# First graph convolution: own-row bias folded into the weights, and another order of work on TensorE, ScalarE and VectorE

## The reference

```python
x = _layernorm(x + _L0_gnn_ref(x, edge_weight, src, dst, ...))
x = _layernorm(x + _L1_gnn_ref(x, edge_index, edge_weight1, ...))   # two transformer convolutions
x = _layernorm(x + _L2_gnn_ref(...))
x = _layernorm(x + _L3_gnn_ref(...))
```

```python
q = (x @ qw + qb).reshape(N, HEADS, CH)          # 8 heads of 16
k = (x @ kw + kb).reshape(N, HEADS, CH)
v = (x @ vw + vb).reshape(N, HEADS, CH)
alpha = jnp.sum(q[dst] * k[src], axis=-1) * SCALE
m = jax.ops.segment_max(alpha, dst, num_segments=N)
a = jnp.exp(alpha - m[dst])
denom = jax.ops.segment_sum(a, dst, num_segments=N)
a = a / denom[dst]
msg = v[src] * a[:, :, None]
out = jax.ops.segment_sum(msg, dst, num_segments=N).reshape(N, HEADS * CH)
return out + x @ sw + sb                          # followed by relu
```

## Time and profile before

| | |
|---|---|
| median of 3 runs (lowest to highest) | 3210.21 us (3208.09 to 3211.15) |
| the profiled execution: own time, span | 3208.55 us, 3206.6 us |
| granted TensorE clock, mean over the span | 0.903 |
| first convolution, 720 to 1190 us: VectorE busy | 454.83 of 470 us |
| the same: TensorE, ScalarE, GpSimd busy | 431.81, 285.16, 166.08 us |
| the same: granted clock, DMA share, GB/s | 1.00, 0.65, 196 |

### The profile page before, as it was taken

One profiled execution on the slowest core, in us unless ns is written; L12 is line 12 of the kernel. 1 busy time (PEld: TensorE's weight loads), 2 busy tenths in 40 slices (PEclk: granted clock), 3 DMA queues, 4 the chain that ended last, 5 costly groups with the idle time before them and its releaser, 6 DMA issues. The chain is left out here.

```text
span 3206.6 us, 46374 instructions
## 1 busy us (share of the span) xinstructions
PE 2528.0 (79%) x14129; PEld 1744.9 (54%) x14129; DVE 2643.1 (82%) x3326; ACT 2089.0 (65%) x3677; POOL 1868.2 (58%) x1771
## 2 busy tenths in 40 slices
PE   7899999959999987888888699999999752445500
PEld 3466666636666654666666466776777541224400
DVE  6599999969999996999999557988888756999910
ACT  0167677636665656999999589999999753555500
POOL 4477777623333326777776466555555007777776
PEclk9999999979999998999999899999999855667855
DMA  7356676656666656777777347889888548885211
GB/s 212 110 187 218 216 228 219 210 166 201 197 200 196 200 169 187 235 232 234 233 230 227 112 144 196 216 208 224 216 220 205 152 113 258 277 276 146 84 40 39
DMA packets 495087, 611.79 MB, mean 191 GB/s; under 512 B 66865, under 2 KB 284651, under 8 KB 494716
## 3 DMA queue, kind: packets, MB, share of 16 engines
q1 hardware_dynamic: 433030, 495.63, 51.3%
q0 software_dynamic: 56480, 111.88, 13.1%
q10 hardware_dynamic: 5334, 1.32, 0.2%
HBM read 391.94 MB, written 220.55 MB: 191 GB/s over the span
## 5 line engine op out<-in xcount | busy, mean ns | idle before, releaser
L775 POOL DMA_INDIRECT c_xs<-table_x,src_row x196 | 185.0, 944 | 302.6 <-PE c_psT L916 249.4
L1815 POOL DMA_INDIRECT f_rows<-table_x,src_row x196 | 227.8, 1162 | 227.8 <-POOLq L1216 168.4
L1295 POOL DMA_INDIRECT g_xd_xs<-table_x,dst_row x196 | 200.0, 1021 | 260.9 <-PE g_psT L1363 167.5
L765 POOL DMA_INDIRECT c_xs<-table_h,src_row x196 | 221.3, 1129 | 121.2 <-issue 78.9
L497 POOL DMA_INDIRECT xs<-in_x,src_i x196 | 227.1, 1159 | 86.6 <-issue 55.5
L482 POOL DMA_INDIRECT xd<-in_x,dst_i x196 | 216.5, 1104 | 94.0 <-issue 47.9
L1295 POOL DMA_INDIRECT g_xd_xs<-table_x,src_row x196 | 206.5, 1053 | 59.7 <-issue 59.7
L1822 POOL DMA_INDIRECT out<-f_rows,end_i x196 | 197.4, 1007 | 62.4 <-issue 62.4
L1867 PE MATMUL f_psT<-w_ident,f_rows 128*128 128x128 f32 x196 | 48.9, 397 | 219.9 <-DVE f_rows L1960 219.9
L765 POOL DMA_INDIRECT c_xd<-table_h,dst_row x196 | 185.0, 944 | 59.7 <-issue 59.7
L1368 PEld LDWEIGHTS g_psP<-w_center,g_turns 128*128 128x128 f32 x1568 | 185.2, 193 | 49.8 <-ACT g_turns L1504 28.5
(11 more groups left out here) (330 smaller groups left out, 8588.6 us busy)
## 6 DMA issues: line engine op xcount, KB each, us to landing
g_share<-shares SPq DMA_DIRECT2D x196, 192.0 KB
xn<-in_x SPq DMA_DIRECT2D x49, 512.0 KB
table_x<-xo SPq DMA_DIRECT2D x49, 512.0 KB, 2.9
table_x1b<-xb SPq DMA_DIRECT2D x49, 512.0 KB, 4.9
c_xn<-table_x SPq DMA_DIRECT2D x49, 512.0 KB
table_h<-c_xo SPq DMA_DIRECT2D x49, 512.0 KB
c_xn<-table_h SPq DMA_DIRECT2D x49, 512.0 KB
c_x1r<-table_x1b SPq DMA_DIRECT2D x49, 512.0 KB
```

Source lines behind the costliest of these rows:

```text
L765: pool.indirect_dma_start(out=quarters(rows[:, s, :])[j], out_offset=None, in_=table, in_offset=edge_index(columns, now.n, j)).then_inc(la ...
L775: pool.indirect_dma_start(out=quarters(xs[:, s, :])[j], out_offset=None, in_=table, in_offset=edge_index(h.src_row, now.n, j)).then_inc(sr ...
L1295: pool.indirect_dma_start(out=quarters(xd_xs[:, s, k, :])[j], out_offset=None, in_=table, in_offset=edge_index(columns, now.n, j)).then_in ...
L1815: pool.indirect_dma_start(out=quarters(rows[:, n, :])[j], out_offset=None, in_=table, in_offset=edge_index(h.src_row, n, j)).then_inc(src_ ...
```

## The change

Own-row bias. A constant 1.0 is added to every value of the turned node rows (`bias=1.0` in the copy out of PSUM), and the own-row weight becomes `s0_lifted` = `s0` + (`s_b0` - column sums of `s0`) / 128. Since every row that the convolution reads has mean zero, (x + 1) @ `s0_lifted` is x @ `s0` + `s_b0`. VectorE's two additions and the array `pre` go; ScalarE takes the relu straight out of PSUM, one half at a time (`store_nodes`), half 0 in the tile's own step and half 1 in the next. The set-up gets one matmul (column sums) and two small VectorE operations for the new weight.

Order. On TensorE q comes right behind the first turn, the edge rows of tile n - 2 move behind k, the own rows of half 0 ahead of the turn of half 1, the scores ahead of the values, and the own rows of half 1 to the end. On VectorE `kq` moves ahead of `pv`, `den` and `num`. ScalarE's step becomes a function of its own. SyncE and GpSimd keep their order; SyncE's store now waits for both halves. In `layer2` the first of two adjacent matmuls now counts as well, and the two waits on it count double.

```diff
@@ setup, VectorE and TensorE
+            dve.wait_ge(columns_summed, 1)
+            link(nc.vector.tensor_tensor(h.s_b0[:, :], h.s_b0[:, :], psm[:, P:2 * P], ALU.subtract))
+            link(nc.vector.scalar_tensor_tensor(out=h.s0_lifted[:, :], in0=h.s_b0[:, :], scalar=1.0 / P,
+                                                in1=h.w["s0"][:, :], op0=ALU.mult, op1=ALU.add))
...
+            pe.wait_ge(loaded, n_loads[0])
+            nc.tensor.matmul(psm[:, P:2 * P], ones[:, :], h.w["s0"][:, :], start=True, stop=True).then_inc(columns_summed, 1)
@@ conv, SyncE
-                    sp.wait_ge(out_ready, last.n + 1)
+                    sp.wait_ge(out_ready, 2 * last.n + 2)
@@ conv, TensorE
-                wait(pe, pren_ready, 2 * now.n - 1 + k)
+                wait(pe, pren_ready if layer else out_ready, 2 * now.n - 1 + k)
...
-                    if soon:
-                        turn_dst(soon)
-                if old:
-                    edge_products(old)
                 if now:
                     pe.wait_ge(d_filled, now.n + 1)
                     wait(pe, kq_ready, now.n)
                     nc.tensor.matmul(psQ[:, :], w_q[:, :], xdT[:, now.at(t_slots), :],
                                      start=True, stop=True).then_inc(q_ready, 1)
+                if soon and now:
+                    turn_dst(soon)
+                if now:
                     turn_spread(1, now, xn[:, s, 0, :], node_landed[s], 16 * (now.half + 1))
                     pe.wait_ge(q_sb, now.n + 1)
                     nc.tensor.matmul(psQ[:, :], w_k[:, :], xsT[:, s, :], start=True, stop=True).then_inc(k_ready, 1)
+                if old:
+                    edge_products(old)
+                if now:
+                    own_rows(now, 0)
                     turn_spread(2, now, xn[:, s, 1, :], node_landed[s], 16 * (now.half + 1))
-                    own_rows(now, 0)
+                    alike(now)
                     values(now)
                     own_rows(now, 1)
-                    alike(now)
@@ conv, ScalarE
+            def keep_nodes(now, k):
+                act.wait_ge(turned, 3 * now.n + 2 + k)
+                wait(act, en_ready, 2 * now.n - 3 + k)
+                nc.scalar.activation(xnT[:, now.slot, k, :], psT[0][:, :], ACT.Copy, bias=1.0).then_inc(turned_sb, 1)
+
+            def store_nodes(tile, k):
+                act.wait_ge(en_ready, 2 * tile.n + 1 + k)
+                wait(act, node_stored[tile.slot], 16 * tile.half)
+                nc.scalar.activation(xo[:, tile.slot, k, :], psE[k][:, :], ACT.Relu).then_inc(out_ready, 1)
...
-                    act.wait_ge(pren_ready, 2 * now.n + 2)
-                    wait(act, node_stored[s], 16 * now.half)
-                    nc.scalar.activation(xo[:, s, 0:2, :], pre[:, s, 0:2, :], ACT.Relu).then_inc(out_ready, 1)
@@ conv, VectorE (times_q holds the old code of kq; for layer 1 it stays where it was)
+                if spread and now:
+                    times_q(now)
...
-                    for k in range(2):
-                        dve.wait_ge(en_ready, 2 * now.n + 1 + k)
-                        nc.vector.tensor_tensor(by_row(pre[:, now.slot, k, :]), by_row(psE[k][:, :]),
-                                                s_bias[:, :].rearrange("p (o f) -> p o f", o=1).to_broadcast([P, 4, P]),
-                                                ALU.add).then_inc(pren_ready, 1)
```

More of the change, by code:

```diff
@@ L792, in conv @@
         to_rows = h.w["ident"] if layer == 0 else h.w["center"]
-        s_bias = h.s_b0 if layer == 0 else h.s_b1c
+        w_own = h.s0_lifted if layer == 0 else h.s1c
         b_q, b_k, b_v = h.col(f"q_b{layer}"), h.col(f"k_b{layer}"), h.b_vs[:, layer:layer + 1]
@@ L930, in own_rows @@
                 pe.wait_ge(turned_sb, per_tile * (now.n + 1) - 1 + k)
-                wait(pe, pren_ready, 2 * now.n - 1 + k)
+                wait(pe, pren_ready if layer else out_ready, 2 * now.n - 1 + k)
                 for o, x in zip(quarters(psE[k]), quarters(xnT[:, now.slot, k, :])):
-                    ins = nc.tensor.matmul(o, x, w_s[:, :], start=True, stop=True)
+                    ins = nc.tensor.matmul(o, x, w_own[:, :], start=True, stop=True)
                 ins.then_inc(en_ready, 1)
@@ L1032, in step, with step_spread @@
+            def step_spread(t):
+                now, last, old = t.tile(0), t.tile(1), t.tile(2)
+                if now:
                     act.wait_ge(turned, 3 * now.n + 1)
                     wait(act, v_ready, now.n - 1)
-                    nc.scalar.activation(xsT[:, s, :], psT[0][:, :], ACT.Copy).then_inc(turned_sb, 1)
-                elif now:
+                    nc.scalar.activation(xsT[:, now.slot, :], psT[0][:, :], ACT.Copy).then_inc(turned_sb, 1)
+                    keep_q(now)
+                if last:
+                    store_nodes(last, 1)
+                if now:
+                    keep_nodes(now, 0)
+                if last:
+                    act.wait_ge(u_ready, last.n + 1)
+                    wait(act, pv_ready, last.n)
+                    wait(act, den_ready, last.n)
+                    nc.scalar.activation(p[:, :], u[:, :], ACT.Exp).then_inc(p_ready, 1)
+                    act.wait_ge(dropm_ready, last.n + 1)
+                    wait(act, num_ready, last.n)
+                    nc.scalar.activation(c[:, :], dropm[:, :], ACT.Exp).then_inc(c_ready, 1)
+                if old:
+                    keep_edges(old)
+                if now:
+                    store_nodes(now, 0)
+                    keep_nodes(now, 1)
+                if last:
+                    act.wait_ge(den_ready, last.n + 1)
+                    wait(act, rden_ready, last.n)
+                    nc.scalar.activation(lnd[:, :], den[:, last.slot, :], ACT.Ln).then_inc(lnd_ready, 1)
+                    act.wait_ge(lnd_ready, last.n + 1)
+                    wait(act, agg_ready, last.n)
+                    nc.scalar.activation(rden[:, :], lnd[:, :], ACT.Exp, scale=-1.0).then_inc(rden_ready, 1)
@@ L1036, in step @@
+            def step(t):
+                now, last, (g, a, b) = t.tile(0), t.tile(1), t.group(1)
+                if now:
                     s = now.slot
@@ L1043, in step @@
                         nc.scalar.activation(dst, psT[k][:, :], ACT.Copy).then_inc(turned_sb, 1)
-                if layer and g:
+                if g:
                     if a == 0:
@@ L1063, in step @@
                     nc.scalar.activation(p[:, :], u[:, :], ACT.Exp).then_inc(p_ready, 1)
-                if spread and old and not now:
-                    keep_edges(old)
                 if now:
                     for k in range(2):
-                        act.wait_ge(turned, per_tile * (now.n + 1) - 1 + k)
+                        act.wait_ge(turned, 4 * now.n + 3 + k)
                         wait(act, en_ready, 2 * now.n - 3 + k)
-                        nc.scalar.activation(xnT[:, s, k, :], psT[0 if spread else k][:, :],
-                                             ACT.Copy).then_inc(turned_sb, 1)
-                if layer and g:
+                        nc.scalar.activation(xnT[:, s, k, :], psT[k][:, :], ACT.Copy).then_inc(turned_sb, 1)
+                if g:
                     norm_scale(nc, act, h, g, a, b, var, lnv, rstd, var_ready, lnv_ready, rstd_ready, out_ready)
@@ L1083, in step @@
                     nc.scalar.activation(rden[:, :], lnd[:, :], ACT.Exp, scale=-1.0).then_inc(rden_ready, 1)
-                if layer and g:
+                if g:
                     scale_rows(t, g, a, b, 3, 12).then_inc(out_ready, 1)
-                if now and not layer:
-                    act.wait_ge(pren_ready, 2 * now.n + 2)
-                    wait(act, node_stored[s], 16 * now.half)
-                    nc.scalar.activation(xo[:, s, 0:2, :], pre[:, s, 0:2, :], ACT.Relu).then_inc(out_ready, 1)
-            run_steps(2, step)
+            run_steps(2, step_spread if spread else step)
         @block.vector
@@ L1112, in _, with times_q @@
                 fill_dst(Tile(0, 0))
+            def times_q(now):
+                dve.wait_ge(k_ready, now.n + 1)
+                dve.wait_ge(q_sb, now.n + 1)
+                wait(dve, a_ready, now.n)
+                nc.vector.scalar_tensor_tensor(out=kq[:, :], in0=psQ[:, :], scalar=b_k, in1=q[:, :],
+                                               op0=ALU.add, op1=ALU.mult).then_inc(kq_ready, 1)
             def add_x1(t, g, k):
@@ L1176, in step @@
                                                  ALU.mult, ALU.add).then_inc(num_ready, 1)
[L1177 to L1182, removed]
+                if now and not spread:
+                    times_q(now)
                 if last:
@@ L1424, in _ @@
                     wait(pe, shares_ready, done)
-                    nc.tensor.matmul(psA[0:32, 0, :], att_a[:, :], zl[:, :], start=True, stop=True)
+                    nc.tensor.matmul(psA[0:32, 0, :], att_a[:, :], zl[:, :], start=True, stop=True).then_inc(a_ready, 1)
```

(2 more changed lines are left out.)

19 lines of the change are left out of this document (6 added, 13 removed).

## The result

| | before | after |
|---|---|---|
| median, measured side by side (4 runs each) | 3210.04 us | 3169.38 us |
| ratio, 95% interval | | 0.9873 (0.9860 to 0.9885) |
| profiled execution: own time, span | 3208.55, 3206.6 us | 3169.91, 3168.1 us |
| granted clock, mean | 0.903 | 0.904 |

The change makes the kernel faster by 40.7 us; forecast were 46, and a median of 3164.

A forecast was written before the change was run, and what follows sets the result against it. VectorE bounded the kernel before; after the change the store-load loop would, at 9.34 us a tile. Gains of 43.2 and 2.9 us, 46.1 together, take 3208.55 to 3162.5, a median of 3164 us; range 3143 to 3189.

The forecast's parts named there:

- VectorE's share: VectorE's work in a tile of the first convolution: 9.05 us after the change, against a tile of 10.24 before.
- The load as bound: Likeliest case, chance 0.52: the next tile's node-row load, queued behind SyncE's store, sets the pace at 9.34 us a tile.
- T + 2.69: When SyncE's store leaves, in us after T, the start of a tile's first turn on TensorE; before the change 1.89.
- the landing: Time from SyncE's store until the next tile's node rows have arrived: 8.95 us taken, 7.48 to 9.74 considered.
- the loop over two tiles: Store to landing 8.95, rest of TensorE's tile 7.03, T to store 2.69: 18.67 us, 9.34 a tile.
- The size of the gain: Gain over the 48 tiles of the stage: 0.90 us each, 43.2 us in all.
- The later-landing rival: Node rows land 9.74 us after the store, as in the slow tile: gain 27.4 us, median 3183, chance 0.14.
- TensorE's share: TensorE's work in a tile, 8.75 us: below VectorE's 9.05, so not the bound alone, with 0.3 us to spare.
- The ends: First and last tile of the stage: waits of 1.75 and 1.15 us go, together 2.9 us gained.
- The set-up: Two new small VectorE operations hidden behind a 0.83 us wait for TensorE; uncovered 0.66 us; the new matmul at worst 0.86.
- VectorE sets the pace before: In the kernel before, VectorE, 97% busy, bounds the 10.24 us tile; what is taken off it is gained until something else is late.
- The fit for a DMA: 2.0 us plus bytes by 436 GB/s: 3.2 us for the node-row load, which would be hidden; the prediction found the trace disagreed.

The follow-up runs named there:

- sending it 0.7 us sooner behind the store: Against the changed kernel, SyncE stores the edge rows ahead of its wait for the node rows' store, not behind that store: 3152.85 us, 0.9825.
- the store later still: Against the changed kernel, ScalarE takes the relu of the second half after p and c instead of right behind q: 3245.52 us, 1.0119.
- the bias alone: Kernel before, with the lifted weight, no additions and each half's relu out of PSUM at the end of ScalarE's step, all orders old: 3207.52 us, 1.0001.

## Why the prediction was right, and where it was not

- **VectorE's share, 9.05 us a tile**: the tiles that do not wait for the load take 9.03, with the wait for `rden` of 0.18 ahead of `agg`, as the last tile of the kernel before had shown.
- **The load as bound**: right. The store left at T + 2.69 as summed, the landing was 8.87 (8.95 taken), and two tiles took 18.64 us (18.67 summed). The wait comes in about every second tile, since the loop spans two; that it would be shared evenly, some 0.6 us a tile, was wrong (0.95 in 24 tiles of 45). Moving the load ahead of the store brought 27 us, and sending it 0.7 us sooner behind the store 17, as the loop over two tiles has it; the store later still cost 76, there by a loop that closes in one tile.
- **The size of the gain**: 48 x (10.24 - 9.52) = 34.6 us from the tiles, where 43.2 were forecast. The mis-sized term is the landing. I took one value from an ordinary tile; over the 25 waiting turns of the changed kernel it runs from 8.0 to 11.9 us, 9.2 in the mean, and late landings are not made good by early ones, since VectorE's 9.03 is the floor. One tile alone cost 14.37 - 9.34 = 5.0 us, 4.80 - 3.09 = 1.7 of it at the lower clock. The later-landing rival was thus part of the truth in some tiles.
- **TensorE's share**, 8.75 summed, was 0.17 short: its tile without a wait takes 909.01 - 900.09 = 8.92. It changed nothing here, since 9.05 and the load lie above it, but it is what remains once the load is out of the way.
- **The ends**: 2.9 us forecast. From the stage's first instruction to the first `m` it is 20.4 us in place of 22.9, and from the last `m` to the next stage 15.4 in place of 16.4: 2.5 and 1.0, 3.5 together.
- **The set-up**: forecast hidden. The convolution's first instruction comes 1.0 us later than before, but with the same set-up it came between 678.6 and 680.5 us in the seven experiments, and at 678.3 in the one trace before. All eight are later than that one, by 0.3 to 2.2 us; whether the set-up costs so much is not settled.
- **What was wrong**: the prediction said that VectorE sets the pace before, and that what is taken off it is gained. It is not: the bias alone gained nothing (1.0001). The pace before was that of the loop through `kq`, the scores, the edge rows, q and `p`, and VectorE's own work stood 0.28 us under it; the wait for `p` in every tile, which an engine that sets the pace alone does not have, was the sign. It was the other half of the change that took this loop down, which the prediction did not price. That the gain came out near the forecast is luck in this step: both halves were in the change.
- **The fit for a DMA** of the Trainium skill ("DMA: Bandwidth & Descriptors", "Anatomy of one DMA — SWDGE (gpsimd) path"), stated for GpSimd's path, would have hidden the load; taken over to SyncE's queue it does not hold: the load landed 911.65 - 905.35 = 6.3 us after its own issue, where the fit gives an estimate of 3.2.

## What to carry to other kernels

Where an engine is 97% busy, look for the loop that is as long or longer before crediting what is taken off it, and take even a short wait that stands in every tile as its sign: of two limits close together, taking down one gives next to nothing. When an instruction moves, ask which DMA waits for it and which loads the issuing engine sends only behind that DMA; here a relu of 0.6 us, moved three places later, cost 76 us, more than the 48 x 1.20 = 58 us of work that the change removed. Loads that need nothing from a store belong ahead of it.

## What the runs showed of the hardware

A wait of 3.78 us on TensorE was followed by a granted clock of 0.53 to 0.62 for four microseconds and a tile of 14.4 us, as shown above; behind the next longest wait for that load, 2.72 us, it stayed at 1.00, as the window behind it and the turn that waited show:

```profile
846.00:847.00 1.00, 1.00 (x6) 0.52 (x5) 0.08 (x1) 0.95 (x2) 0.77 (x1) 1.00 0.98 156
```

```profile
845.36 0.66 PE L923 MATMUL c_psT<-w_ident,c_xn 128*128 128x128 f32 x4 [2.72 <-DMA c_xn<-table_x]
```

No run was made to tell what decides between the two. That a load's landing spreads from 8.0 to 11.9 us at a DMA share of 0.72 was more than I had read from the kernel before, where nothing waited for it.
